# Diagonal products of two heads in one product of 64x128 columns, the unwanted blocks masked when they are collected, and the gram product in another PSUM bank

## The chip, the cores and the metric

The kernel runs on one core of one Trainium2 chip. Its time is the device time in microseconds (us) of one execution, given as the median of several. Lower is better. The core has TensorE (PE, whose weight loads the profile lists as PEld), VectorE (DVE), ScalarE (ACT), GpSimd (POOL) and SyncE (SP, which here issues the DMAs).

## What is computed

A block of a network: layer norm with modulation, a Mamba2 state-space layer, a gated residual, and after it layer norm and a linear layer with binarized weights. The change touches the chunked scan of the state-space layer. Cut to what matters:

```python
def ssd_chunk_scan(X, dA, Bm, Cm, chunk):
    # X: (b,l,h,p), 64 heads h of p = 16; Bm, Cm: (b,l,g,n), 8 groups of n = 64, each shared by 8 heads
    A_cum = jnp.cumsum(A, axis=-1)
    Lm = jnp.exp(segsum(A))                     # lower triangular decays inside a chunk
    Y_diag = jnp.einsum('bcshn,bczhn,bhcsz,bczhp->bcshp', Cm, Bm, Lm, X)
    decay_states = jnp.exp(A_cum[..., -1:] - A_cum)
    states = jnp.einsum('bcshn,bhcs,bcshp->bchpn', Bm, decay_states, X)
    ...
    Y_off = jnp.einsum('bcshn,bchpn,bhcs->bcshp', Cm, states, state_decay_out)
    return (Y_diag + Y_off).reshape(b, l, h, p)
```

Batch is 4, length 512, model width 512, inner width 1024; all in float32.

## The kernel before

The kernel cuts the scan into chunks of 64 tokens. A **step** n is one pair of groups (4 pairs) and one batch element (4): 16 steps, 16 heads and 512 tokens each. A step has 4 **units** u of 128 tokens, that is two chunks c; there are 64 units. The main loop runs over v from -2 to 63 and, in each v, over four slots `sl`. Every engine has its own program, written out in the same slots, and semaphores join them; nothing is scheduled by a tool. In one iteration v PE does, in order: at slot 0 the diagonal and off-diagonal products of unit v and the states and gram products of unit v+1; at slots 1, 2 and 3 the turn of x, two decay products and the turn of B for unit v+2; and in each of the slots 1 to 3 half a projection (`project`, line 1196: six products of 512 columns) of the input for a later step. Between them, in some units, lie turns of weights (`weights`, line 1291).

A unit goes through these stages. `decay` (L1205) makes exponents in bank DB, ACT's `exponent` (L1365) turns them into M; `gram` (L1274) makes C times B for both groups; DVE's `mix` (L1476) multiplies M by it, two operations of 512 columns. `turn_x` (L1214) puts x with tokens on partitions into bank XT, ACT's `spread` (L1373) copies it to Xp, POOL's `weigh` (L1581) scales it to Xw. `turn_b` (L1223) turns B into bank GB and ACT's `copy_b` (L1378) copies it to BTs. `states` (L1247) makes each chunk's own state; DVE's `update` (L1506, L1509) adds it to the faded one that POOL makes (`fade`, L1591). `diagonal` (L1261) multiplies M by Xp; `offdiagonal` (L1234) multiplies the state by C. DVE's `collect` (L1491, L1492, L1494) scales the off-diagonal part by `ea` and adds the diagonal part, into y1, and POOL's `sum_up` (L1609) adds y1 to t1.

A head has only 16 columns and PE writes in strips of 32 partitions. So Xp holds each head in 32 columns, 16 of them zeros: an even head lies in the lower half, an odd one in the upper. Two products, of an even and an odd head, are summed in one strip (`start=(e == 0), stop=(e == 1)`); the zeros keep them apart. The pair of PSUM banks YS holds, in each bank: columns 0 to 127 the diagonal result, 128 to 255 the off-diagonal one, 256 to 383 the states, 384 to 447 the gram. The products with 64 rows use half of the array's rows, and the half (c or q) also decides the bank.

DVE's program in iteration v is: slot 1 `update(v+1, 0)` and `collect(v)`; slot 2 `update(v+1, 1)` and `mix(v+1)` twice; besides, in slots that a table sets, `silu` (L1467) and the three operations of `convolve` (L1446) on a projected tile. A projection k may start when `silu` of tile k-3 has freed its bank (three banks A). The diagonal of v+1 waits for the mixes of v+1.

## Time and profile before

| | |
|---|---|
| time, median of 3 runs | 672.53 us (671.93 to 673.36) |
| span of the profiled execution | 672.7 us |
| mean granted clock of TensorE | 0.976 |
| busy: PE | 624.5 us, 93% |
| busy: DVE | 521.1 us, 77% |
| busy: ACT, POOL | 379.5 us, 56%; 357.3 us, 53% |
| diagonal products (L1261) | 4096 MATMUL records |

The profiled execution's own time is its span. Busy times of PE count products whose ends are modelled and which overlap, so they say where PE works and not how full it is. A product of float32 operands appears as two MATMUL records and two LDWEIGHTS records.

### The profile page before, as it was taken

To read this page: it belongs to the slowest core of one execution; us is meant where nothing else is said; L and a number is where in the kernel's file an instruction comes from. 1 tells how busy PE (TensorE), PEld (TensorE's weight loads), DVE (VectorE), ACT (ScalarE), POOL (GpSimd) and SP (SyncE) were. 2 spreads that over 40 slices of the span, in tenths; PEclk is the share of its full clock that TensorE was granted. 3 is DMA by queue.
4 is the path that set the end of the run, shared out by engine and by line. 5 is a ranking of instruction groups with operands and counts; after the bars stand their busy time and mean duration, and the time that the engine had idled before them with its cause. 6 is when DMAs were issued, how large, how long until landed. Compare 5 with 4: busy or idle time off the path is not lost.

```text
span 672.7 us, 21311 instructions
## 1 busy us (share of the span) xinstructions
PE 624.5 (93%) x8371; PEld 491.5 (73%) x8371; DVE 521.1 (77%) x947; ACT 379.5 (56%) x834; POOL 357.3 (53%) x416
## 2 busy tenths in 40 slices
PE   3887977999999999999999999999978989999995
PEld 1664756777777878778777878777866767888884
DVE  6698689888687887887778878778698466677766
ACT  3776444546646455646545564756664527665555
POOL 5674211626555463754734655447564645767652
PEclk9698889999999999999999999999997999999999
DMA  9743111242321231322122253222323634444411
GB/s 288 234 146 115 47 38 52 70 157 75 117 70 38 97 107 52 101 69 87 67 71 73 78 168 118 69 101 70 101 69 106 215 125 141 145 153 126 126 48 62
DMA packets 61914, 70.52 MB, mean 105 GB/s; under 512 B 13972, under 2 KB 33460, under 8 KB 61816
## 3 DMA queue, kind: packets, MB, share of 16 engines
q1 hardware_dynamic: 61816, 69.17, 32.1%
q8 instruction: 67, 1.10, 0.7%
q14 instruction: 31, 0.25, 0.1%
HBM read 54.45 MB, written 14.70 MB: 103 GB/s over the span
## 4 chain that ended last, share of the span: by engine, by line
PE 75%; DVE 11%; issue 4%; POOL 4%; ACT 3%; DMA 1%; SPq 0%; POOLq 0%; DVEq 0%; ACTq 0%
PE bank L1196 35%; PE bank L1962 11%; PE pair L1261 7%; PE bank L1205 4%; PE bank L1995 3%; PE pair L1234 3%; PE bank L1291 2%; DVE m_cv L1446 2%; PE bank L1214 2%; PE pair L1247 2%; POOL h_lo L428 1%; DVE chain L589 1%; DVE chain L596 1%; DVE m_M L1476 1%; PE pair L1274 1%
## 5 line engine op out<-in xcount | busy, mean ns | idle before, releaser
L1446 DVE SCALAR_TENSOR_TENSOR m_cv<-bank,gpc,m_cv 128x511 f32<-128x511 f32 (+2 forms) x192 | 143.4, 747 | 38.3 <-ACT m_cv L1353 33.6
L1196 PE MATMUL bank<-h_hi,w_hi 128*128 128x512 f32 x384 | 164.6, 429 | 3.6 <-DVE m_xs L1467 1.9
L1196 PE MATMUL bank<-h_hi,w_lo 128*128 128x512 f32 x384 | 153.1, 399 | 0.0
L1196 PE MATMUL bank<-h_lo,w_hi 128*128 128x512 f32 x384 | 152.5, 397 | 0.4 <-issue 0.4
L1353 ACT ACTIVATE m_cv<-bank,gpc 128x512 f32<-128x512 f32 x96 | 72.0, 750 | 79.8 <-PE bank L1196 79.4
L1365 ACT ACTIVATE m_M<-bank 128x512 f32<-128x512 f32 x128 | 76.0, 594 | 66.5 <-PE bank L1205 65.3
L1591 POOL TENSOR_TENSOR m_S<-m_S,m_cd 128x128 f32<-128x128 f32 x96 | 40.0, 416 | 136.9 <-DVE m_S L1509 71.3
L1196 PEld LDWEIGHTS bank<-h_hi,w_hi 128*128 128x128 f32 x384 | 74.0, 193 | 24.4 <-issue 5.5
L1581 POOL TENSOR_TENSOR m_Xw<-m_Xp,wend 128x256 f32<-128x256 f32 x64 | 39.8, 622 | 87.7 <-ACT m_Xp L1373 87.7
L1196 PEld LDWEIGHTS bank<-h_hi,w_lo 128*128 128x128 f32 x384 | 73.4, 191 | 17.5 <-issue 0.6
L1196 PEld LDWEIGHTS bank<-h_lo,w_hi 128*128 128x128 f32 x384 | 73.9, 192 | 12.1 <-issue 0.3
L1476 DVE TENSOR_TENSOR m_M<-m_M,pair 128x512 f32<-128x512 f32 x128 | 81.7, 679 | 0.2 <-issue 0.2
L1261 PEld LDWEIGHTS pair<-m_M,m_Xp 64*32 64x32 f32 x4096 | 45.7, 105 | 25.9 <-issue 25.5
L1261 PE MATMUL pair<-m_M,m_Xp 64*32 64x64 f32 x4096 | 56.3, 225 | 7.9 <-DVE m_M L1476 7.9
L1360 ACT ACTIVATE bank<-m_cv 128x512 f32<-128x512 f32 x96 | 58.4, 608 | 6.3 <-DVE m_cv L1446 6.3
L1816 POOL TENSOR_TENSOR t_y_lo<-h_lo_place,t_y_hi 128x1024 fp32r<-128x1024 f32 x16 | 39.1, 2445 | 39.6 <-ACT t_y_hi L1762 35.1
L1205 PE MATMUL bank<-R,Lm 84*128 84x512 f32 x128 | 57.3, 448 | 1.5 <-ACT m_M L1365 1.5
L1962 PE MATMUL bank<-h_hi,t_y_hi 128*128 128x512 f32 x128 | 51.5, 403 | 1.3 <-POOL t_y_lo L1816 1.3
L1962 PE MATMUL bank<-h_hi,t_y_lo 128*128 128x512 f32 x128 | 50.7, 396 | 0.0
L1962 PE MATMUL bank<-h_lo,t_y_hi 128*128 128x512 f32 x128 | 50.7, 396 | 0.0
L1467 DVE SCALAR_TENSOR_TENSOR m_gate<-bank,m_cv 128x512 f32<-128x512 f32 x32 | 22.1, 690 | 33.3 <-ACT bank L1360 33.3
L1602 POOL TENSOR_TENSOR m_t<-m_xs,m_dd 128x512 f32<-128x512 f32 x32 | 40.6, 1291 | 4.0 <-DMA m_dd<-dd_scratch 3.1
(184 smaller groups left out, 1260.0 us busy)
## 6 DMA issues: line engine op xcount, KB each, us to landing
m_ea<-ea_scratch SPq DMA_DIRECT2D x32, 256.0 KB
m_dd<-dd_scratch SPq DMA_DIRECT2D x32, 256.0 KB
y_scratch<-m_t SPq DMA_DIRECT2D x16, 512.0 KB, 3.4
h_lo_place<-y_scratch SPq DMA_DIRECT2D x16, 512.0 KB, 4.7
p_wm<-in_L_wmod_dram SPq DMA_DIRECT2D x6, 1024.0 KB, 6.9
m_wraw<-in_L_attn_in_proj_w_dram SPq DMA_DIRECT2D x18, 256.0 KB, 3.1
w_lo_place<-in_L_attn_input__dram SPq DMA_DIRECT2D x16, 256.0 KB, 4.9
out_dram<-t_o SPq DMA_DIRECT2D x16, 256.0 KB, 2.4
```

The lines of the kernel that those rows point to most:

```text
L1196: ins = pe.matmul(A[k % 3][:, :], w[:, t, kc, :], h[:, n % NB, kc, :], start=(m == 0), stop=(m == 11))
L1205: pe.matmul(DB[:, :], s.Lm[:, u % 2, q, :], s.R[:, u % 2, q, :], start=True, stop=True).then_inc(d_done, 1)
L1261: ins = pe.matmul(YS[32 * j:32 * j + 32, c, q * Q:(q + 1) * Q], Xp[half, u % 2, HG * q + h, :], M[half, u % 2, q, h * Q:(h + 1) * Q], star ...
L1353: act.activation(cv[:, k % 3, :], A[k % 3][:, :], ACT.Identity, scale=scale, bias=bias).then_inc(lin_done, 1)
L1360: act.activation(A[k % 3][:, :], cv[:, k % 3, :], ACT.Tanh).then_inc(tanh_done, 1)
L1365: act.activation(M[:, u % 2, q, :], DB[:, :], ACT.Exp).then_inc(exp_done, 1)
L1446: ins = dve.scalar_tensor_tensor(out=cv[:, k % 3, lag:], in0=A[k % 3][:, 0:L - lag], scalar=s.gpc[:, gp, o:o + 1], in1=cv[:, k % 3, lag:], ...
L1476: dve.tensor_tensor(m, m, g, ALU.mult).then_inc(m_done, 1)
L1581: pool.tensor_tensor(Xw[:, :, :].rearrange("p q (j e d) -> p (q j) e d", e=2, d=HD), src, w, ALU.mult).then_inc(xw_done, 1)
L1591: pool.tensor_tensor(S1[:, c, :].rearrange("p (h d) -> p h d", h=HG), S[:, (m - 1) % 4, :].rearrange("p (h d) -> p h d", h=HG), cd[:, b // ...
L1602: pool.tensor_tensor(t1[:, q, :], xs[:, n % 2, q, :], dd[:, q, :], ALU.mult).then_inc(t1_done, 1)
L1962: ins = pe.matmul(OB[i][:, :], y[:, i, k, :], w[k], start=(k == 0 and m == 0), stop=(k == KI - 1 and m == 2))
```

## The change

**Diagonal.** Xp loses its padding: `spread` copies 256 columns as they are, 16 to a head. One product takes the 32 columns of two heads as weights and the two heads' 128 columns of M. Its result of 32 partitions by 128 columns has four blocks; the two in which head and head's decays meet are wanted, the other two are not. 16 products of 128 columns take the place of 32 of 64 columns.

**Collecting.** `own_half` is a column of ones and zeros per head's half (two columns: even, odd). `collect` adds the even half's columns times the first, then the odd half's columns times the second, both with a scalar from a column. So there are three operations for two, and four for three in the first unit of a step. y1 is laid out by chunk.

**Banks.** The diagonal result now takes columns 0 to 127 and 256 to 383 in each bank of YS, and the states 384 to 511. The gram moves into bank GB, the turn of B from there into columns 256 to 383 of XT. Both gram halves share one bank now, so q = 1 waits for q = 0 (`g_first`), and PE's order is gram(0), offdiagonal(1), states, offdiagonal(0), gram(1).

```diff
-        ea, y1 = sb("ea", [P, 2, 2, L]), sb("y1", [P, 2, 2, L])
+        ea, y1 = sb("ea", [P, 2, 2, L]), sb("y1", [P, 2, NC, 2, Q])
-        Xp, Xw = sb("Xp", [P, 2, 2 * HG, 32]), sb("Xw", [P, 2, HG * HD])
+        Xp, _, Xw = sb("Xp", [P, 2, 2 * HG * HD]), sb("pad4", [P, 2 * 2 * HG * HD]), sb("Xw", [P, 2, HG * HD])
...
+        dve.wait_ge(konst, 3)
+        dve.tensor_reduce(s.own_half[:, :], s.ident[:, :].rearrange("p (j e d) -> p e j d", e=2, d=HD), AX.XY, ALU.add)
...
-        pool.wait_ge(t_pe, 16)
-        pool.memset(s.Xp[:, :, :, :], 0.0).then_inc(zeroed, 1)
...
-                pe.transpose(GB[:, 0:P], Bt[:, n % 2, tok(u)], s.ident[:, :]).then_inc(bt_done, 1)
+                pe.wait_ge(xp_done, u + 1)
+                pe.transpose(XT[:, 2 * P:3 * P], Bt[:, n % 2, tok(u)], s.ident[:, :]).then_inc(bt_done, 1)
...
             def diagonal(u):
...
                 for q in range(2):
-                    for e in range(2):
-                        for j in range(4):
-                            for c in range(2):
-                                half, h = slice(64 * c, 64 * c + 64), 2 * j + e
-                                ins = pe.matmul(YS[32 * j:32 * j + 32, c, q * Q:(q + 1) * Q], Xp[half, u % 2, HG * q + h, :],
-                                                M[half, u % 2, q, h * Q:(h + 1) * Q], start=(e == 0), stop=(e == 1))
+                    for j in range(4):
+                        for c in range(2):
+                            half, first = slice(64 * c, 64 * c + 64), q * P + 32 * j
+                            ins = pe.matmul(YS[32 * j:32 * j + 32, c, 2 * P * q:2 * P * q + 2 * Q], Xp[half, u % 2, first:first + 32],
+                                            M[half, u % 2, q, 2 * j * Q:2 * (j + 1) * Q], start=True, stop=True)
...
+            def gram(u, q):
+
+                n, group = u // UPS, slice(64 * q, 64 * q + 64)
+                if q == 1:
+                    pe.wait_ge(g_first, u + 1)
+                else:
+                    if u % UPS == 0:
+                        pe.wait_ge(silu_done, TILE_NO[n, 3] + 1)
+                    pe.wait_ge(bt_read, u + 1)
+                    wait(pe, m_done, 2 * u)
                 for c in range(2):
...
+                    ins = pe.matmul(GB[64 * c:64 * c + 64, q * Q:(q + 1) * Q], Bt[group, n % 2, chunk(u, c)],
+                                    Ct[group, n % 2, chunk(u, c)], start=True, stop=True)
+                ins.then_inc((g_first, g_done)[q], 1)
...
                     if v >= 0 and piece_at(slot) is not None:
                         if sl == 3:
-                            pe.wait_ge(xp_done, u + 1)
+                            pe.wait_ge(xp_done, min(u + 1, NU))
+                            pe.wait_ge(bt_read, min(u + 1, NU))
                         weights(piece_at(slot))
...
-                out = Xp[:, u % 2, :, :].rearrange("p (j e) (m d) -> p j (e m) d", e=2, d=HD)[:, :, 0:4:3, :]
-                act.activation(out, XT[:, 0:2 * P].rearrange("p (j e d) -> p j e d", e=2, d=HD), ACT.Copy).then_inc(xp_done, 1)
+                act.activation(Xp[:, u % 2, :], XT[:, 0:2 * P], ACT.Copy).then_inc(xp_done, 1)
...
             def collect(u):
...
-                dve.wait_ge(g_done, min(u + 2, NU))
+                wait(dve, st_done, min(u + 2, NU))
...
                 if i == 0:
...
-                    dve.tensor_copy(dst[:, 0, :, :], own[:, 0, :, :])
+                    dve.tensor_scalar(flat[:, 0:2, :], own[0][:, 0:2, :], s.own_half[:, 0:1], None, ALU.mult).then_inc(yo_scaled, 1)
                 dve.tensor_tensor(dst[:, first:, :, :], off[:, first:, :, :], scale[:, first:, :, :], ALU.mult).then_inc(yo_scaled, 1)
-                dve.wait_ge(yo_scaled, u + 1)
-                dve.tensor_tensor(dst[:, first:, :, :], own[:, first:, :, :], dst[:, first:, :, :], ALU.add).then_inc(y1_done, 1)
+                dve.wait_ge(yo_scaled, 2 * u + n + 2)
+                dve.scalar_tensor_tensor(out=flat[:, 2 * first:, :], in0=own[0][:, 2 * first:, :], scalar=s.own_half[:, 0:1],
+                                         in1=flat[:, 2 * first:, :], op0=ALU.mult, op1=ALU.add).then_inc(yo_scaled, 1)
+                dve.wait_ge(yo_scaled, 2 * u + n + 3)
+                dve.scalar_tensor_tensor(out=flat, in0=own[1], scalar=s.own_half[:, 1:2], in1=flat,
+                                         op0=ALU.mult, op1=ALU.add).then_inc(y1_done, 1)
```

The new code has its own line numbers. PE's program before, at slot 0 of the iteration whose diagonal belongs to unit 29 (`pair` is YS, `bank` any other PSUM bank, in brackets the semaphores that a row waits for):

```order
L1261 MATMUL pair<-m_M,m_Xp 32x64 [waits m_m_done,m_xp_done,m_s_new,m_y1_done]
L1261 MATMUL pair<-m_M,m_Xp 32x64 x31
L1234 MATMUL pair<-m_Ct,m_S 64x64 x8
L1247 MATMUL pair<-m_Xw,m_BTs 64x128 [waits m_bt_read,m_xw_done,m_s_new]
L1247 MATMUL pair<-m_Xw,m_BTs 64x128
L1274 MATMUL pair<-m_Ct,m_Bt 64x64 [waits m_bt_read]
L1274 MATMUL pair<-m_Ct,m_Bt 64x64 x3
L1196 MATMUL bank<-h_hi,w_hi 128x512 [waits p_h_lo_dve,m_silu_done,p_h_lo_pool,p_w_pool]
```

PE's program after, at the same place:

```order
L1262 MATMUL pair<-m_M,m_Xp 32x128 [waits m_m_done,m_xp_done,m_s_new,m_y1_done]
L1262 MATMUL pair<-m_M,m_Xp 32x128 x15
L1277 MATMUL bank<-m_Ct,m_Bt 64x64 [waits m_m_done,m_bt_read]
L1277 MATMUL bank<-m_Ct,m_Bt 64x64
L1235 MATMUL pair<-m_Ct,m_S 64x64 x4
L1249 MATMUL pair<-m_Xw,m_BTs 64x128 [waits m_bt_read,m_xw_done,m_s_new]
L1249 MATMUL pair<-m_Xw,m_BTs 64x128
L1235 MATMUL pair<-m_Ct,m_S 64x64 x4
L1277 MATMUL bank<-m_Ct,m_Bt 64x64 [waits m_g_first]
L1277 MATMUL bank<-m_Ct,m_Bt 64x64
```

The 32 products have become 16, one gram pair stands ahead of the off-diagonals, the other behind them, and the states stand between the two halves of the off-diagonals.

DVE's program before, around `collect` of unit 28, the first of its step (L1506 and L1509 are `update`, L1476 is `mix`, L1467 is `silu`):

```order
L1509 TENSOR_TENSOR m_S<-m_S,pair 128x128 [waits m_g_done,m_s_part,m_yd_done,m_st_done]
L1491 COPY m_y<-pair 128x2x64 [waits m_ea_ready1,m_g_done,m_y_out,m_yo_done,m_yd_done]
L1492 TENSOR_TENSOR m_y<-pair,m_ea 128x2x64
L1494 TENSOR_TENSOR m_y<-pair,m_y 128x2x64 [waits m_yo_scaled]
L1467 SCALAR_TENSOR_TENSOR m_xs<-bank,m_cv 128x512 [waits m_t1_done,m_xt_done,m_tanh_done]
L1509 TENSOR_TENSOR m_S<-m_S,pair 128x128 [waits m_g_done,m_s_part,m_yd_done,m_st_done]
L1476 TENSOR_TENSOR m_M<-m_M,pair 128x512 [waits m_g_done,m_exp_done] x2
```

DVE's program after, at the same place:

```order
L1525 TENSOR_TENSOR m_S<-m_S,pair 128x128 [waits m_yo_done,m_s_part,m_yd_done,m_st_done]
L1503 TENSOR_SCALAR m_y<-pair,p_own_half 128x128 [waits m_ea_ready1,m_st_done,m_y_out,m_yo_done,m_yd_done]
L1504 TENSOR_TENSOR m_y<-pair,m_ea 128x128
L1506 SCALAR_TENSOR_TENSOR m_y<-pair,p_own_half,m_y 128x128 [waits m_yo_scaled]
L1509 SCALAR_TENSOR_TENSOR m_y<-pair,p_own_half,m_y 128x256 [waits m_yo_scaled]
L1477 SCALAR_TENSOR_TENSOR m_xs<-bank,m_cv 128x512 [waits m_t1_done,m_xt_done,m_tanh_done]
L1525 TENSOR_TENSOR m_S<-m_S,pair 128x128 [waits m_yo_done,m_s_part,m_yd_done,m_st_done]
L1486 TENSOR_TENSOR m_M<-m_M,bank 128x512 [waits m_g_done,m_exp_done] x2
```

Between the first update and the SiLU of x stand four operations where three stood, the last one over 256 columns. In the other units of a step it is three for two, all of 256 columns.

## Rows read from the trace of the kernel before

**Rows 1.** The page: span, and the chain that ended last, by engine

```profile
span 672.7 us, 21311 instructions
...
PE 75%; DVE 11%; issue 4%; POOL 4%; ACT 3%; DMA 1%; SPq 0%; POOLq 0%; DVEq 0%; ACTq 0%
```

**Rows 2.** Busy time by stretch: length, engines with instructions, granted clock, DMA

```profile
core 0: us, PE busy (x) PEld busy (x) DVE busy (x) ACT busy (x) POOL busy (x), PEclk, DMA share, GB/s
91.10:119.80 28.70, 23.30 (x359) 17.86 (x357) 27.90 (x49) 14.27 (x31) 6.11 (x11) 1.00 0.15 52
262.00:276.00 14.00, 14.00 (x238) 11.16 (x238) 11.83 (x24) 8.71 (x22) 9.62 (x13) 1.00 0.14 42
489.10:502.20 13.10, 10.33 (x138) 7.81 (x138) 12.86 (x27) 8.91 (x21) 7.48 (x11) 1.00 0.22 76
503.00:512.00 9.00, 8.30 (x116) 6.53 (x103) 8.13 (x16) 3.55 (x9) 4.71 (x5) 0.62 0.04 8
```

**Rows 3.** Timeline of PE: start, length, line, instruction, shapes, count of records

```profile
300.15 0.86 PE L1261 MATMUL pair<-m_M,m_Xp 64*32 64x64 f32 x64
300.94 0.46 PE L1234 MATMUL pair<-m_Ct,m_S 64*64 64x64 f32 x16
...
306.80 0.86 PE L1261 MATMUL pair<-m_M,m_Xp 64*32 64x64 f32 x64
...
313.66 1.00 PE L1261 MATMUL pair<-m_M,m_Xp 64*32 64x64 f32 x64
314.59 0.46 PE L1234 MATMUL pair<-m_Ct,m_S 64*64 64x64 f32 x16
```

**Rows 4.** Busy by stretch, instructions of L1261 alone; (x) is how many are in flight

```profile
300.15:300.23 0.08, 0.07 (x8) 0.08 (x16) 1.00 0.00 0
...
300.34:300.40 0.06, 0.06 (x32) 0.06 (x17) 1.00 0.00 0
...
300.48:300.80 0.32, 0.32 (x51) 0.32 (x31) 1.00 0.00 0
```

**Rows 5.** The same view, instructions of L1247 alone

```profile
301.22:301.33 0.11, 0.10 (x4) 0.11 (x8) 1.00 0.00 0
301.33:301.44 0.11, 0.11 (x8) 0.05 (x4) 1.00 0.00 0
```

**Rows 6.** Timeline of DVE, units 29 and 30

```profile
302.66 0.42 DVE L1492 TENSOR_TENSOR m_y<-pair,m_ea 128x256 f32<-128x256 f32 x1
303.11 0.42 DVE L1494 TENSOR_TENSOR m_y<-pair,m_y 128x256 f32<-128x256 f32 x1
303.45 0.28 DVE L1509 TENSOR_TENSOR m_S<-m_S,pair 128x128 f32<-128x128 f32 x1
303.91 1.28 DVE L1476 TENSOR_TENSOR m_M<-m_M,pair 128x512 f32<-128x512 f32 x2 [0.18 <-issue]
```

**Rows 7.** Groups by form: busy us, mean ns of one, idle before

```profile
L1446 DVE SCALAR_TENSOR_TENSOR m_cv<-bank,gpc,m_cv 128x511 f32<-128x511 f32 x64 | 47.7, 745 | 33.7 <-ACT m_cv L1353 33.6
```

**Rows 8.** Timeline of DVE ahead of the diagonal of unit 29

```profile
294.50 2.32 DVE L1446 SCALAR_TENSOR_TENSOR m_cv<-bank,gpc,m_cv 128x511 f32<-128x511 f32 x3 [1.28 <-ACT m_cv L1353]
...
296.93 0.28 DVE L1491 COPY m_y<-pair 128x128 f32<-128x128 f32 x1
...
297.65 0.68 DVE L1467 SCALAR_TENSOR_TENSOR m_xs<-bank,m_cv 128x512 f32<-128x512 f32 x1
...
298.44 1.27 DVE L1476 TENSOR_TENSOR m_M<-m_M,pair 128x512 f32<-128x512 f32 x2
```

**Rows 9.** Waits of PE: total us, times, longest

```profile
PE pair L1261 <- DVE m_M L1476: 7.9, 5, 3.1
```

**Rows 10.** Timeline of DVE and PE: a bank freed, a projection started

```profile
269.86 0.68 DVE L1467 SCALAR_TENSOR_TENSOR m_xs<-bank,m_cv 128x512 f32<-128x512 f32 x1
...
270.59 0.50 PE L1196 MATMUL bank<-h_hi,w_hi 128*128 128x512 f32 x1
...
298.58 0.48 PE L1196 MATMUL bank<-h_hi,w_hi 128*128 128x512 f32 x1
```

More of the change, by code:

```diff
@@ L1246, in states @@
                         half, group = slice(64 * c, 64 * c + 64), slice(64 * q, 64 * q + 64)
-                        ins = pe.matmul(YS[group, c, 256:384], BTs[half, group], Xw[half, q, :], start=True, stop=True)
+                        ins = pe.matmul(YS[group, c, 384:512], BTs[half, group], Xw[half, q, :], start=True, stop=True)
                 ins.then_inc(st_done, 1)
@@ L1377, in copy_b @@
                 wait(act, st_done, u)
-                act.activation(BTs[:, :], GB[:, 0:P], ACT.Copy).then_inc(bt_read, 1)
+                act.activation(BTs[:, :], XT[:, 2 * P:3 * P], ACT.Copy).then_inc(bt_read, 1)
             def weights(i):
@@ L1401, in scalar @@
             start.scalar(act, linear, tanh)
-            act.wait_ge(start.zeroed, 1)
             for v in range(-2, NU):
```

77 lines of the change are left out of this document (40 added, 37 removed).

## The prediction, made before the changed kernel was run

> **What bounds the kernel now.** I read the page first: the chain that ended last is 75% TensorE and 11% VectorE [rows 1]. That is a mean over stages, so I then read busy times by stretch [rows 2]. There the reader sees two regimes. From 262 to 276 us, which stands for nearly all of the loop (unit 6 at 142 us to unit 56 at 488 us), PE is busy 14.00 of 14.00 us and DVE 11.83: TensorE sets the pace. From 91.1 to 119.8 and from 489.1 to 502.2 us DVE is busy 27.90 of 28.7 and 12.86 of 13.1 us: VectorE sets it (as it does again ahead of unit 6), since the first stretch carries the second half's decay chain and the last one the signs of the FFN weight. The change takes work from TensorE and gives work to VectorE, so the question is how much of each lands in which regime, and whether VectorE has room inside the TensorE-bound one.
>
> **What TensorE saves.** A unit's 32 diagonal products are 64 MATMUL records of 64 columns, from 300.15 until the next block starts at 300.94: 0.79 us [rows 3]. How they run, the counts of records in flight show: eight in the first 0.08 us, thirty-two by 300.40 [rows 4], so eight arrays of 64x32 work at once and each group of eight takes about 0.056 us. That rate isn't held: the second half of the 64 takes from 300.40 to 300.80. Afterwards there are 32 records of 128 columns. Their pace is bounded by the states' products, also 128 columns, where four records start in 0.11 us and the next four 0.11 us later [rows 5], twice the 0.056 of 64 columns. If eight arrays still work at once, 32 records are four groups: the last starts 3 x 0.11 + 0.05 us after the first. From the last start to the next block the trace leaves 0.14 us (300.80 to 300.94), to which the longer stream adds 0.05. Sum 0.57 us, a saving of **0.21 us a unit**. The columns streamed are the same in number; what goes is the slow second half. Bounds: 0.10 if the new order of the block behind costs 0.11 (below), 0.39 if what costs is the record (0.79/64 x 32). I take 0.21, since the pace of 128 columns is read directly. In seven units of the middle the old block takes 0.93 us (313.66 to 314.59) [rows 3], and there 0.14 more goes.
>
> The block behind it has the same products: gram 4, off-diagonal 8, states 4. Before, each kind filled all four arrays of 64x64 at once; now a gram pair fills the two of the upper row half while the off-diagonal four fill the lower, and the other way round at the end. Counted by array the columns are equal, so I cost it at zero if arrays run independently. The new waits on PE I cost at nothing, and name the cover: for m_done the diagonal has just waited; g_first comes with the first gram products and is asked for behind the states and the other off-diagonals; ScalarE copies Xp while PE computes the second decay, and BTs while PE runs half a projection, six products of 512 columns. If that cover went, the half projections queued behind would be late, and with them their activations.
>
> **What VectorE pays.** Each collect gets one more operation and two with a scalar from a column. Before, the two of 256 columns start 0.45 us apart, and the next independent one 0.34 after the second [rows 6]: 0.79 us. The pointer's price: m_cv's operation reads PSUM with such a scalar over 511 columns in 745 ns [rows 7], m_xs's with a constant over 512 in 0.68 [rows 8], so 0.06 us. After: 0.45, then 0.42 + 0.065 + 0.03 (the gap of a dependent operation) = 0.52, then 0.34 + 0.065 = 0.41: 1.38 us, or **+0.59**. In the first unit of a step the three operations are of 128 columns and take 0.72 us (296.93 to 297.65 [rows 8]); with two pointers and a dependent operation of 256 columns more that is +0.13 and +0.52: **+0.65**. Without the pointer's price it is +0.46, which I keep as the lower end.
>
> **Where it lands.** *Start, units 0 to 5:* VectorE-bound except from 120 to 127 us. Collects 0, 1, 2, 4 and 5 lie on its chain: 2 x 0.65 + 3 x 0.59 = 3.1, less one TensorE saving of 0.21: +2.9 us.
>
> *Middle, units 6 to 56, 50 steps.* PE has waited for a mix only five times in 64 units [rows 9]. In three steps of four VectorE is well ahead: the mixes of unit 30 end at 303.91 + 1.28 = 305.19 [rows 6], the diagonal starts at 306.80 [rows 3], and 1.35 us remain after the 0.26 of such a start when it does wait. Each of these steps loses its 0.21: 38 x 0.21 = 8.0, and 7 x 0.14 = 1.0. The fourth is the second unit of a step, 29, 33 and so on. There, from the convolution at 294.50 VectorE runs without a pause through collect of 28 (296.93), SiLU of x (297.65) and the mixes (to 299.71) [rows 8]. Two things wait for it. The projection that takes the freed bank starts at 298.58, 0.25 us after that SiLU ends at 298.33; in unit 25's step it starts 0.05 us after (269.86 + 0.68 to 270.59) [rows 10]. And the diagonal starts at 300.15, 0.43 us after the mixes. Of those 0.26 is again no cover. So of collect's +0.65 only 0.17 to 0.20 is cover here, and nothing in unit 25. The chain begins at an activation before the preceding diagonal, so TensorE's saving doesn't shorten it. The twelve steps lengthen by 0.45 to 0.64 each, which I take at 0.55: +6.6 us. What is late next is m_cv and the mixes of the following unit, with some 0.6 us left of the 1.35. Middle: 6.6 - 8.0 - 1.0 = -2.4 us.
>
> *End:* collects 56 and 57 lie on VectorE's chain again, +1.2; units 61 to 63 save 3 x 0.21 = 0.6; collect 59 before a TensorE wait about +0.1. +0.7 us.
>
> The work at the start costs nothing: own_half's reduction stands ahead of VectorE's wait for the first copy of the decay weight, and is hidden there, and the zeroing of Xp that goes from POOL had idle time behind it. ScalarE's copy and POOL's weighting of 256 columns keep their sizes.
>
> Sum: 2.9 - 2.4 + 0.7 = +1.2 us on a profiled span of 672.7 [rows 1], which is the median of the runs (672.5) within 0.2. **Forecast 673.7 us**: no change that the measurement tells; it tells about 0.2%, 1.35 us.
>
> **Rivals.** *VectorE's extra is cheap (B).* If the pointer costs nothing, the start pays 2.1 instead of 2.9, the middle 12 x 0.36 instead of 6.6, the end 0.3 instead of 0.7: 2.1 + 4.3 - 9.0 + 0.3 = -2.3, **670.2 us**. For it: m_cv's operands also start at odd offsets, which could be its 0.06. Against: its 509 and 511 columns cost the same. Chance 0.18.
>
> *Records cost, not columns (C).* The second half of the 64 records is paced by something per record, for they are no wider than those of the first. If that price holds for all, 32 fewer save 0.39 us a unit: 38 x 0.18 and the end's 0.5 more than above, **666.4 us**. Against it: eight starts in 0.056 us [rows 4]. Chance 0.07. The Trainium skill ("TensorE: Matmul & The Clock Gate", Back-to-back issue gap) gives small products a floor of about 25 ns each. By that the 64 would have taken 1.6 us, where the trace has 0.79 for this tiling, and halving them would save 0.8 us a unit, which I don't believe.
>
> *Arrays don't run apart (D), the slower side.* If PE starts products strictly in order, the states' second product waits for the row half in which the off-diagonals still run, while the other, with only the gram pair, stands idle for one group of 0.11 us; the saving is then 0.10 instead of 0.21 in the 38 steps and four more at the ends: 42 x 0.11 = +4.6, **678.3 us**. Since the forecast already stands at +1.2, it decides from 0.01 us a unit on. For it: nothing in the old order tests unequal halves. Against: eight starts in 0.08 us from products that each are two records on one array [rows 4]. Chance 0.17. The Trainium skill says both: products start in strict order ("TensorE: Matmul & The Clock Gate", Part 3), and arrays work independently ("TensorEngine Tiling (Array Packing)", Key Properties); no run so far decides it.
>
> *Clock (E).* PE now pauses about 0.6 us more per unit in the VectorE-bound stretches. From 489.1 to 502.2 us it was busy 10.33 of 13.1, and from 503 to 512 the granted clock is 0.62, so three quarters of these nine at 1.2 instead of 2.4 GHz [rows 2], which costs up to 3.4 us. One such stretch more, on the path: **676.5 us**. Chance 0.13.
>
> **Numbers.** The forecast (A, its own range 671.5 to 675.8 from the 0.45 to 0.64 of the twelve steps and 0.04 us either way in TensorE's saving) has 0.45, B 0.18, C 0.07, D 0.17, E 0.13. Leaving out C and the far part of D gives 669.3 to 678.0. Of A somewhat more than half lies inside 0.2%. Faster 0.27 (B, C, the edge of A), same 0.34, slower 0.39 (D, E, A's upper part).
>
> **What would show it.** The diagonal block at about 0.57 us from its first record to the gram's, in even groups of eight per 0.11 us; the block behind it unchanged at 0.73 us to the next projection (0.84 under D). Collect at 1.38 us from its first operation to the next. PE idle about 0.5 us once in four units, waiting for m_xs or m_M, where before it was not. Unit 6 about 3 us later than 142.34, unit 56 about where it was. I would be wrong if VectorE's operations with a column scalar cost under 0.45 us, if the block behind the diagonal grows, or if the clock falls elsewhere.

## The result, and the profile after

The changed kernel took **678.12 us** in the median of four runs (676.11 to 681.79), the kernel before beside it 672.71 (671.93 to 673.36): a ratio of 1.0092, interval 1.0063 to 1.0120. The forecast was 673.7 with a range up to 678.0, so the change cost 5.4 us where I expected 1.2. Run again later (e9, six runs), it took 678.10 against 672.49, ratio 1.0072 (1.0047 to 1.0097).

The page of the changed kernel: span, busy times, and the chain that ended last.

```profile
span 679.9 us, 17403 instructions
...
PE 622.1 (92%) x6323; PEld 478.0 (70%) x6323; DVE 554.9 (82%) x1012; ACT 379.8 (56%) x834; POOL 354.6 (52%) x415
...
PE 67%; DVE 17%; issue 6%; ACT 5%; POOL 4%; DVEq 1%; POOLq 0%; ACTq 0%
```

Against [rows 1] the chain has moved from TensorE (75% to 67%) to VectorE (11% to 17%). A share says nothing yet of where. For that I took the first record of a unit's diagonal block (L1261 before, L1262 after) as a milestone and read how far apart the milestones lie in both traces:

| stretch | before | after | difference | forecast |
|---|---|---|---|---|
| start to unit 0 | 94.10 | 96.20 | +2.1 | 0 |
| unit 0 to 6 | 48.24 | 51.39 | +3.15 | +2.9 |
| unit 6 to 8 | 13.52 | 14.71 | +1.2 | -0.4 |
| unit 8 to 56 | 331.76 | 330.56 | -1.2 | -2.0 |
| unit 56 to 63 | 51.69 | 54.75 | +3.1 | +0.9 |
| unit 63 to the end | 133.4 | 132.3 | -1.1 | -0.2 |
| span | 672.7 | 679.9 | +7.2 | +1.2 |

(The forecast's Middle and End are cut at units 8 and 63 here: 48 of its 50 steps hold 36 x 0.21 + 1.0 - 12 x 0.55.) The profiled execution was the longest of the four. At 681.79 us it lies 3.7 us over its kernel's median. In every run of this study the time lies 1.7 to 2.3 us above the span; so the profiled execution of before, with its span of 672.7, must have been about 2 us over its median too. The median's +5.4 is what has to be explained, and the profile's +7.2 holds 1.8 us on top.

**The steady middle.** Busy time by stretch (the columns are those of [rows 2]) from unit 8 to 56, first before the change, then after:

```profile
155.85:487.61 331.76, 331.11 (x5661) 263.06 (x5660) 262.35 (x504) 192.38 (x429) 179.61 (x239) 1.00 0.27 86
```

```profile
162.31:492.87 330.56, 323.12 (x4125) 249.52 (x4124) 287.52 (x553) 192.39 (x429) 179.30 (x239) 1.00 0.27 86
```

And what TensorE waited for in that stretch of the changed kernel (total us, how many times, longest):

```profile
PE bank L1197 <- DVE m_xs L1477: 7.4, 12, 0.9
```

TensorE's busy time falls by 8.0 us and its idle time rises from 0.65 to 7.4: twelve waits in twelve steps, each for SiLU of x, which stands behind the collect. That is the mechanism of the forecast in one view: -8.0 + 6.8 = -1.2.

How the wait comes about shows in VectorE's timeline ahead of unit 29:

```profile
303.29 0.28 DVE L1525 TENSOR_TENSOR m_S<-m_S,pair 128x128 f32<-128x128 f32 x1
303.48 0.35 DVE L1503 TENSOR_SCALAR m_y<-pair,p_own_half 128x128 f32<-128x128 f32 x1
303.74 0.28 DVE L1504 TENSOR_TENSOR m_y<-pair,m_ea 128x128 f32<-128x128 f32 x1
304.06 0.35 DVE L1506 SCALAR_TENSOR_TENSOR m_y<-pair,p_own_half,m_y 128x128 f32<-128x128 f32 x1
304.45 0.48 DVE L1509 SCALAR_TENSOR_TENSOR m_y<-pair,p_own_half,m_y 128x256 f32<-128x256 f32 x1
304.85 0.68 DVE L1477 SCALAR_TENSOR_TENSOR m_xs<-bank,m_cv 128x512 f32<-128x512 f32 x1
```

The collect takes 1.37 us from its first operation to the SiLU, where it took 0.72 [rows 8]: the +0.65 that was forecast for a step's first unit. TensorE's timeline of the same place and of the diagonal blocks of units 28 and 29:

```profile
300.14 0.67 PE L1262 MATMUL pair<-m_M,m_Xp 64*32 64x128 f32 x32
300.74 0.27 PE L1277 MATMUL bank<-m_Ct,m_Bt 64*64 64x64 f32 x2
...
305.58 0.50 PE L1197 MATMUL bank<-h_hi,w_hi 128*128 128x512 f32 x1 [0.35 <-DVE m_xs L1477]
...
307.18 0.67 PE L1262 MATMUL pair<-m_M,m_Xp 64*32 64x128 f32 x32
307.78 0.27 PE L1277 MATMUL bank<-m_Ct,m_Bt 64*64 64x64 f32 x2
...
307.94 0.27 PE L1249 MATMUL pair<-m_Xw,m_BTs 64*64 64x128 f32 x1
307.96 0.22 PE L1235 MATMUL pair<-m_Ct,m_S 64*64 64x64 f32 x1
307.96 0.32 PE L1249 MATMUL pair<-m_Xw,m_BTs 64*64 64x128 f32 x1
...
308.29 0.22 PE L1277 MATMUL bank<-m_Ct,m_Bt 64*64 64x64 f32 x2
308.34 0.23 PE L1235 MATMUL pair<-m_Ct,m_S 64*64 64x64 f32 x2
308.35 0.23 PE L1277 MATMUL bank<-m_Ct,m_Bt 64*64 64x64 f32 x2
308.40 0.22 PE L1235 MATMUL pair<-m_Ct,m_S 64*64 64x64 f32 x1
308.55 0.50 PE L1197 MATMUL bank<-h_hi,w_hi 128*128 128x512 f32 x1
```

The projection waits 0.35 us for the SiLU that ends at 305.53. The diagonal block is 0.60 us long (300.14 to 300.74) where it was 0.79 [rows 3] and 0.57 was forecast. The block behind it, forecast to stay at 0.73, is 0.77 us in unit 29 (307.78 to 308.55): the states' products (L1249) no longer start in even groups but one by one among the off-diagonals (L1235).

**The clock.** What the change lost from unit 6 to 8 is not a wait. Here are the busy times of the changed kernel for the stretch as a whole, then for the part of it in which the clock was down:

```profile
147.59:162.31 14.72, 14.71 (x173) 11.40 (x173) 12.20 (x23) 5.51 (x12) 5.62 (x7) 0.88 0.20 59
147.90:151.30 3.40, 3.40 (x62) 2.61 (x41) 3.33 (x7) 0.00 (x0) 1.31 (x2) 0.50 0.18 64
```

TensorE is busy throughout, and its granted clock is 0.50, that is 1.2 instead of 2.4 GHz, from 147.9 to 151.3. Just before, from 145.10 to 147.59, it had stood idle for the mixes of unit 6. Before the change that pause was 1.65 us (140.69 to 142.34). The diagonal of unit 6, with the pause ahead of it in brackets, first before the change, then after:

```profile
142.34 0.36 PE L1261 MATMUL pair<-m_M,m_Xp 64*32 64x64 f32 x19 [1.65 <-DVE m_M L1476]
```

```profile
147.59 0.92 PE L1262 MATMUL pair<-m_M,m_Xp 64*32 64x128 f32 x32 [2.49 <-DVE m_M L1486]
```

Before the change the same stretch ran at full clock:

```profile
142.34:155.85 13.51, 13.51 (x236) 10.82 (x236) 11.12 (x21) 5.51 (x12) 5.57 (x7) 1.00 0.22 76
```

The profiled executions as wholes show the clock too: mean 0.976 before, 0.962 after.

### The profile page after: what moved, and what is told of

Its sections match the earlier page's. It is cut to its first block, busy times and chain, and to the rows that moved or that the text cites. A ratio compares the mean times of both kernels' runs of the same rounds, so it can differ in the third digit from the quotient of the medians.

```text
span 679.9 us, 17403 instructions
## 1 busy us (share of the span) xinstructions
PE 622.1 (92%) x6323; PEld 478.0 (70%) x6323; DVE 554.9 (82%) x1012; ACT 379.8 (56%) x834; POOL 354.6 (52%) x415
## 4 chain that ended last, share of the span: by engine, by line
PE 67%; DVE 17%; issue 6%; ACT 5%; POOL 4%; DVEq 1%; POOLq 0%; ACTq 0%
PE bank L1197 31%; PE bank L1980 11%; DVE m_cv L1456 5%; PE pair L1262 4%; PE bank L2013 3%; PE bank L1206 3%; PE bank L1294 2%; PE bank L1277 2%; PE pair L1235 2%; ACT m_cv L1365 2%; PE bank L1215 2%; PE pair L1249 1%; DVE m_xs L1477 1%; DVE m_M L1486 1%; PE pair L767 1%
## 5 line engine op out<-in xcount | busy, mean ns | idle before, releaser
L1197 PE MATMUL bank<-h_hi,w_hi 128*128 128x512 f32 x384 | 166.7, 434 | 13.2 <-DVE m_xs L1477 11.8
L1456 DVE SCALAR_TENSOR_TENSOR m_cv<-bank,gpc,m_cv 128x511 f32<-128x511 f32 (+2 forms) x192 | 143.2, 747 | 27.8 <-ACT m_cv L1365 23.2
L1197 PE MATMUL bank<-h_lo,w_hi 128*128 128x512 f32 x384 | 154.4, 402 | 0.0
L1486 DVE TENSOR_TENSOR m_M<-m_M,bank 128x512 f32<-128x512 f32 x128 | 81.6, 679 | 0.0
L1980 PE MATMUL bank<-h_hi,t_y_hi 128*128 128x512 f32 x128 | 51.5, 403 | 1.3 <-POOL t_y_lo L1834 1.3
L1235 PE MATMUL pair<-m_Ct,m_S 64*64 64x64 f32 x896 | 49.2, 227 | 0.0
L1262 PE MATMUL pair<-m_M,m_Xp 64*32 64x128 f32 x2048 | 43.5, 279 | 5.6 <-DVE m_M L1486 5.6
L1277 PE MATMUL bank<-m_Ct,m_Bt 64*64 64x64 f32 x512 | 41.4, 239 | 1.9 <-ACT p_grow L742 1.9
L1262 PEld LDWEIGHTS pair<-m_M,m_Xp 64*32 64x32 f32 x2048 | 26.1, 107 | 23.5 <-issue 23.5
```

Of the source, the lines that this page charges most:

```text
L1197: ins = pe.matmul(A[k % 3][:, :], w[:, t, kc, :], h[:, n % NB, kc, :], start=(m == 0), stop=(m == 11))
L1235: ins = pe.matmul(YS[strip, q, P + Q * c:P + Q * c + Q], S[group, (2 * u + c - 1) % 4, strip], Ct[group, n % 2, chunk(u, c)], start=True, ...
L1262: ins = pe.matmul(YS[32 * j:32 * j + 32, c, 2 * P * q:2 * P * q + 2 * Q], Xp[half, u % 2, first:first + 32], M[half, u % 2, q, 2 * j * Q:2 ...
L1277: ins = pe.matmul(GB[64 * c:64 * c + 64, q * Q:(q + 1) * Q], Bt[group, n % 2, chunk(u, c)], Ct[group, n % 2, chunk(u, c)], start=True, sto ...
L1456: ins = dve.scalar_tensor_tensor(out=cv[:, k % 3, lag:], in0=A[k % 3][:, 0:L - lag], scalar=s.gpc[:, gp, o:o + 1], in1=cv[:, k % 3, lag:], ...
L1486: dve.tensor_tensor(m, m, g, ALU.mult).then_inc(m_done, 1)
```

## The experiments

The theory after the comparison: VectorE's longer collect costs what was forecast, directly; TensorE's saving is smaller, since the block behind the diagonal grew; and TensorE's longer pauses pull its clock down where before they didn't. The rivals: that TensorE's new order, not the collect, gives the saving back (O), and that the clock's falls have nothing to do with the change (chance). Each kernel ran beside the kernel before; ratios are to it, with their 95% intervals. "Unit 8 to 56" and the like are read from each kernel's trace as above.

**e1, TensorE's part alone.** collect is as cheap as before; the rows of odd heads get the unwanted block instead of their own.

```diff
-    dve.tensor_scalar(flat[:, 0:2, :], own[0][:, 0:2, :], s.own_half[:, 0:1], None, ALU.mult)
+    dve.tensor_copy(dst[:, 0, :, :], own[:, 0, :, :])
...
-    dve.scalar_tensor_tensor(out=flat[:, 2 * first:, :], in0=own[0][:, 2 * first:, :], ...)
-    dve.scalar_tensor_tensor(out=flat, in0=own[1], scalar=s.own_half[:, 1:2], in1=flat, ...)
+    dve.tensor_tensor(dst[:, first:, :, :], own[:, first:, :, :], dst[:, first:, :, :], ALU.add)
```

> The changed kernel, whose collect is as cheap as before: three operations without a column scalar, on the even heads' products alone; the odd heads' own-chunk products are computed but not added to y, so the output lacks them. It shows TensorE's part of the change alone. Theory V (the longer collect on VectorE is what costs, directly and through the clock that falls when TensorE pauses): the start's 3.1 us and the twelve lengthened steps go, and the 0.14 us a unit that TensorE's block behind and diagonal save together stays in some 45 units: 672.5 - 6 to 7 = 666 us (664 to 668). Rival O (the new order on TensorE with its waits gives the saving back wherever the collect stands): 671 to 673 us, and the step of the steady group stays at its length of the change.

Measured: 668.74 us against 673.32, ratio 0.9927 (0.9897 to 0.9957), or -4.9 us. Unit 8 to 56 took 325.58 us (-6.2) and unit 0 to 6 47.96 (-0.3). Rival O falls: without the collect's cost the saving stays. The middle saved what was expected (0.14 us in some 45 units); the time is 1 to 2 us above the expected one, and the trace shows where 1.2 of them lie: the clock fell behind the pause before unit 6 here as well (143.2 to 146.6 us; from unit 6 to 8 14.76 us against 13.52), at a pause of 1.88 us. So it isn't the collect alone that brings the fall about.

**e2, VectorE's part alone.** On the kernel before: the column scalars (1.0 and 0.0) and one operation more; y1 is laid out by chunk as in the change.

```diff
-    dve.tensor_tensor(dst[:, first:, :, :], own[:, first:, :, :], dst[:, first:, :, :], ALU.add)
+    dve.scalar_tensor_tensor(out=sums[:, first:, :], in0=whole[:, first:, :], scalar=s.own_half[:, 0:1], ...)
+    dve.scalar_tensor_tensor(out=sums, in0=whole, scalar=s.own_half[:, 1:2], in1=sums, op0=ALU.mult, op1=ALU.add)
```

> The kernel before, whose collect costs what the change's does: the copy and the addition get a column scalar of 1.0, and one more dependent operation of 256 columns adds 0.0 times the product; TensorE's instructions are those of before. Theory V: the start pays 3.1 us, twelve steps 0.45 to 0.64 each (6.6), the end 1.3, and nothing is saved: 672.5 + 11 = 683.5 us (681 to 687, the upper part if TensorE's pauses lower its clock more often). Rival S (VectorE's extra is mostly covered in the middle, and the change loses only by the clock and by TensorE's own waits): 675 to 678 us.

Measured: 684.32 us, ratio 1.0178 (1.0148 to 1.0208), or +12.0 us; 11 was expected, and S falls. Unit 0 to 6: 51.70, +3.5 (forecast 3.1 without TensorE's saving). Unit 6 to 8: 16.36, +2.8, with the clock down from 147.1 us for 6.8 us. Unit 8 to 56: 337.57, +5.8, or 0.48 for each of twelve steps. The busy times of that stretch, and TensorE's wait in it, the same twelve as in the changed kernel:

```profile
163.64:501.21 337.57, 331.91 (x5661) 263.20 (x5660) 288.17 (x553) 192.21 (x429) 179.25 (x239) 1.00 0.27 85
```

```profile
PE bank L1199 <- DVE m_xs L1470: 5.7, 12, 0.7
```

The two halves add up roughly: -4.9 and +12.0 make +7.1, the whole change made +5.4 and +5.6 in its two measurements. In the middle the sum is -6.2 + 5.8 = -0.4 and the whole -1.2.

**e3, SiLU ahead of the collect.** The wait is for SiLU of x; so take it out from behind the collect.

```diff
+    if sl == 1:
+        for k in due(slot, SILU_LAG):
+            silu(k)
     if sl == 1 and v >= 0:
         collect(v)
...
-    for k in due(slot, SILU_LAG):
-        silu(k)
+    if sl != 1:
+        for k in due(slot, SILU_LAG):
+            silu(k)
```

> The changed kernel with the SiLU that falls due in a collect's slot put ahead of that collect on VectorE; the work is the same. The projection that waits for its freed bank then no longer stands behind the collect. Theory V with the bank as the binding wait in the second units of the steps (15 such waits, up to 2.4 us in all of the change's trace): 0.2 to 0.5 us in each of twelve steps, 2.5 to 6 us less than the change: 672 to 676 us. Rival M (the mixes, which keep their place behind both, bind just as much): 677 to 678 us, as the change. A loss, 679 us or more, if the SiLU waits for its tanh and holds the collect up.

Measured: 676.71 us, ratio 1.0066 (1.0042 to 1.0091), not to be told from the change (1.0072 and 1.0092). Unit 8 to 56 took 329.70, 0.9 less than the change. TensorE's waits in that stretch:

```profile
PE pair L1262 <- DVE m_M L1486: 8.4, 12, 0.9
```

Twelve again, but now ahead of the diagonal, that is behind the mixes: rival M in the main, though the time lies between the two that were expected. As in the forecast, two things wait on one chain, and freeing one shows the other.

**e4 and e10, the gram's move alone.** e4 is the kernel before with the gram in GB, the turn of B in XT and the new order on TensorE with its waits; diagonal and collect as before.

```diff
-    offdiagonal(v)
-    states(v + 1)
-    gram(v + 1)
+    gram(v + 1, 0)
+    offdiagonal(v, 1)
+    states(v + 1)
+    offdiagonal(v, 0)
+    gram(v + 1, 1)
```

> The kernel before with the change's other half alone: gram product in the other bank, turn of B in the bank of x's, and the new order behind the diagonal block; the diagonal products stay as before, 64 of 64 columns with padding, and so does collect. Theory K (the skewed halves cost the 0.05 us that the block behind grew by, in every unit that TensorE bounds): 45 to 55 units x 0.05 = +2 to +3: 675 us. Rival D (row halves held back by the order, 0.11 us): 677 to 679 us. Rival N (the growth comes from the longer last diagonal products, not from the order): 672 to 673 us.

Measured: 675.50 us, ratio 1.0041 (1.0014 to 1.0067), or +2.8 us; theory K's figure. Unit 29's block behind the diagonal, from the first gram record to the projection:

```profile
304.62 0.28 PE L1277 MATMUL bank<-m_Ct,m_Bt 64*64 64x64 f32 x2
...
304.79 0.27 PE L1248 MATMUL pair<-m_Xw,m_BTs 64*64 64x128 f32 x1
304.80 0.22 PE L1234 MATMUL pair<-m_Ct,m_S 64*64 64x64 f32 x1
...
305.40 0.50 PE L1196 MATMUL bank<-h_hi,w_hi 128*128 128x512 f32 x1
```

0.78 us, with the same single starts as in the changed kernel, though the diagonal products are the old ones: N falls. What the new order has that the old had not is an unequal load: a gram pair uses each of the two arrays of the upper rows once, the four off-diagonals use each of those of the lower rows twice, and the states' products behind them came in turn from upper, lower, upper, lower rows. e10 turns the two loops and changes nothing else:

```diff
-    for q in range(2):
-        for c in range(2 if u % UPS < UPS - 1 else 1):
+    for c in range(2 if u % UPS < UPS - 1 else 1):
+        for q in range(2):
```

> The kernel of e4 (before, with the gram product moved and the new order, padded diagonal products) with the states' products row half by row half as in e5. Theory K (the alternation of row halves in strict order makes the block 0.05 us longer and is all that the move costs): from the diagonal block to the projection back from 1.562 to 1.515 us, unit 8 to 56 back to 332 us, the time to that of the kernel before, 673.4 us. Rival (the move costs by something else too, its other waits or the turn of B in the other bank): 674.5 to 675.5 us, unit 8 to 56 over 333 us.

The same block in e10:

```profile
300.54 0.27 PE L1277 MATMUL bank<-m_Ct,m_Bt 64*64 64x64 f32 x2
...
300.70 0.28 PE L1248 MATMUL pair<-m_Xw,m_BTs 64*64 64x128 f32 x2
300.71 0.28 PE L1234 MATMUL pair<-m_Ct,m_S 64*64 64x64 f32 x4
...
301.26 0.50 PE L1196 MATMUL bank<-h_hi,w_hi 128*128 128x512 f32 x1
```

Pairs again, and 0.72 us: the loop order makes the 0.05 to 0.06, that is shown. How it does is not. I had counted, for e5, that each product waits for the one ahead of it. But an array's next product of 64 columns starts 0.11 us or more behind the one before it, so that count gives rival D's growth of 0.11. And in the rows of the changed kernel above, records of the second gram pair start at 308.29, while off-diagonal records, which stand ahead of it in the program, start at 308.34 and 308.40.

Unit 8 to 56 went from e4's 334.26 to 330.70. Not all of those 3.6 us are the order: 1.6 of e4's are two single waits (1.0 us that nothing in the profile explains, 0.6 for a load of Lm). TensorE's busy time in the stretch fell by 1.9 us. The whole time, 674.23 us (ratio 1.0026, 1.0006 to 1.0046), overlaps with e4's interval. By the ratios the order costs 1.0 us, within the intervals. e10's time lies between what theory K and its rival gave, 0.26% over the kernel before, while its unit 8 to 56 is shorter than either said, 1.1 us under that of before: whether the move costs anything else stays open. One growth does remain: in a step's first unit the stretch from the diagonal's start to the next projection is 1.51 us before and 1.56 in e4 and e10 alike (means of twelve). No run isolates its cause.

**e5, the same two lines turned in the changed kernel.**

> The changed kernel with one thing turned: the four products of the states come row half by row half (both column halves of the upper rows, then both of the lower) and no longer alternate between the row halves. Counted by 64x64 arrays with starts in strict order, the change's order makes the block behind the diagonal 6 groups of 0.056 us long, since the upper right array waits behind a product of the lower rows; this order makes it 5, as it was before the change. Theory K (that is the 0.05 us by which the moved gram product lengthens each unit, +2.5 us between units 8 and 56): the block shrinks by 0.05 us, the stretch from unit 8 to 56 by 2.0 to 2.7 us, the time to about 675.5 us. Rival G (the growth comes from something else of the move, such as the turn of B in x's bank or the last gram product's own start): no difference from the change, 678 us.

Measured: 675.49 us, ratio 1.0038 (1.0017 to 1.0058), about 2.6 us under the change by the medians. The trace gives less: unit 8 to 56 took 329.60, 0.96 less than the change. Cut by unit of the step (means over units 8 to 55), the stretch from a diagonal's start to the next projection is 1.372, 1.437, 1.376 and 1.502 us in the change (first to fourth unit) and 1.372, 1.391, 1.376 and 1.454 in e5. So the loop order delays two units of four, those where the off-diagonals and the next unit's states are both complete (a step's first unit has half the off-diagonals, and behind its third come half the states). 12 x 0.094 = 1.1 us is what the loop order costs in the middle. My 2.0 to 2.7 took it for every unit.

**e6, keep TensorE busy in two pauses.** Six products of 128x512 into DB, ahead of the diagonals of units 2 and 6, whose results nobody reads.

```diff
+    if v in (2, 6):
+        pe.wait_ge(exp_done, 2 * (v + 2))
+        for _ in range(6):
+            pe.matmul(DB[:, :], s.w_hi[:, 0, 0, :], s.h_hi[:, 0, 0, :], start=True, stop=True)
     if v >= 0:
         diagonal(v)
```

> The changed kernel with six products of 128x512 put on TensorE, into a bank that is free, ahead of the diagonal blocks of units 2 and 6, where TensorE otherwise waits 2.4 to 2.5 us for the mixes; their results are overwritten unread. Theory E (TensorE's pause in the VectorE-bound start lets its clock fall to half right behind it, at 117.2 and 147.9 us of the change's trace, and the second of these costs 1.2 us in the step from unit 6 to 8, 14.7 against 13.5 us before): from 6 to 8 13.4 to 13.6 us, the kernel 1.2 us shorter, 676 to 677 us. Rival (the clock falls at instants that have nothing to do with these two pauses): 14.7 us stay, 678 us.

Measured: 674.66 us, ratio 1.0032 (1.0014 to 1.0051), less than the 676 to 677 that I expected. The pause before unit 6 in TensorE's timeline, and the busy times of the stretch behind it:

```profile
142.85 1.66 PE L1321 MATMUL bank<-h_hi,w_hi 128*128 128x512 f32 x6 [0.47 <-ACT m_M L1381]
144.86 0.67 PE L1262 MATMUL pair<-m_M,m_Xp 64*32 64x128 f32 x32 [0.35 <-DVE m_M L1490]
```

```profile
144.86:158.05 13.19, 13.19 (x172) 10.29 (x172) 12.10 (x23) 5.50 (x12) 5.62 (x7) 1.00 0.18 59
```

13.19 us at clock 1.00 against 14.71 at 0.88: 1.5 us. It is also 0.33 under the 13.52 of before, near the 0.4 that the forecast had for this stretch. The chance theory falls for this place: in all six traces with the long collect on VectorE and this pause left open (after, e2, e3, e5, e8, e9; pauses of 2.35 to 3.03 us) the clock fell within 0.4 us of its end. From unit 0 to 6 another 1.05 us went (50.34 against 51.39); the falls at 117.2 and 147.9 us are gone, one at 102.3 is still there. This 1.05 is less sure: e5's trace, without the six products, has no fall at 117 us either and 50.93 us. So work that does nothing makes the kernel 2.6 us faster by its trace; the medians say 3.4, the ratios 2.7 to 4.0. The median of the mean granted clock is 0.9765 in e6's twelve runs and 0.9695 in the change's six of e9.

**e7, the odd half taken off VectorE.** The experiments point to a version: keep the merged products, mend the order, and let engines with room do the extra operation. ScalarE scales the odd half out of PSUM, GpSimd adds it; ScalarE reads the banks first, and VectorE waits for that.

```diff
+    def odd_half(u):
+        ...
+        act.activation(odd[:, u % 2, :].rearrange("p (r s) -> p r s", s=Q), own, ACT.Copy, scale=s.own_half[:, 1:2])
+    def add_odd(u):
+        ...
+        pool.tensor_tensor(flat, flat, odd[:, u % 2, :], ALU.add)
...
-    dve.scalar_tensor_tensor(out=flat, in0=own[1], scalar=s.own_half[:, 1:2], in1=flat, op0=ALU.mult, op1=ALU.add)
```

> The changed kernel with the states' order of e5 and with the odd heads' half of collect taken off VectorE: ScalarE scales it out of PSUM into SBUF ahead of VectorE's reads of that bank, and GpSimd adds it to y. VectorE keeps three operations a collect as before, one or two of them with a column scalar. Theory V (VectorE's longer collect is what costs): what e1 showed (4.9 us under the kernel before) plus the 2.5 us of the states' order, less 0.5 to 1 for the column scalars: 666 to 667 us. Rival W (VectorE's first operation behind the diagonal block now waits for ScalarE's, 0.4 us and what is queued ahead of it, and this lands on the path in most units as the collect did): 674 to 680 us.

Measured: **667.59 us** against 673.37, ratio 0.9929 (0.9904 to 0.9953): 5.8 us faster than the kernel before and 10 faster than the change, a little over the 666 to 667 that I expected. Busy times from the page, and the two new operations in the groups by line:

```profile
PE 615.5 (92%) x6323; PEld 473.3 (71%) x6323; DVE 529.0 (79%) x948; ACT 406.4 (61%) x898; POOL 400.4 (60%) x479
```

```profile
L1400 ACT ACTIVATE m_odd<-pair,p_own_half 128x256 f32<-128x256 f32 x64 | 30.4, 475 | 51.3 <-PE pair L1241 51.2
...
L1622 POOL TENSOR_TENSOR m_y<-m_y,m_odd 128x256 f32<-128x256 f32 x64 | 47.5, 743 | 4.6 <-DVE m_y L1526 4.6
```

VectorE is busy for 529.0 us where it was 554.9; ScalarE took 30 and GpSimd 48, and both have room. Rival W, that VectorE's first read now waits on ScalarE, stays small: between units 8 and 56 it takes 6.95 us on average from a step's first unit to its second, against 7.46 in the change and 6.88 before.

**e8, e5 and e3 together.**

> The changed kernel with both reorderings: the states by row half (e5) and the SiLU ahead of the collect (e3). If their gains add (2.5 and 1.7 us): 674 us, still no gain over the kernel before. If TensorE's shorter block only lengthens the wait for the mixes in VectorE-bound units, a little less: 675 us. Rival: one of them was chance between runs, 676.5 us.

Measured: 677.80 us (674.19 to 680.92), ratio 1.0073 (1.0048 to 1.0099). Its trace has the shortest middle of all kernels with the long collect (328.70 us), and yet the median is no better than the change's, where 674 to 675 was expected if both gains were real. So the medians confirm neither e3's gain nor, since e8 holds that edit too, e5's 2.6 us; what holds is the 1.1 us that the block's rows show. Its first unit starts at 96.30 us and its clock fell at 35.3, 117.2 and 147.9 us as in the change. Of differences of 1 to 2 us between two medians here no edit need be the cause.

**e9, the change again.**

> The changed kernel once more, unaltered, for more executions and a second profile: its four first ones spread over 5.7 us (676.11 to 681.79), and their times went with their mean granted clocks. Theory E (the extra half-clock stretches in the part before the first unit, at 117 and 148 us, and at 510 to 530 us are partly chance of the execution): the median 676.5 to 677.5 us, the profile's first unit not at 96.2 but nearer to 94.1 to 94.5 us, from unit 8 to 56 330.6 us to within 0.3 as before, from 6 to 8 again 14.7. Rival (all that the first profile shows belongs to the change): 678 us and the same unit times.

Measured: 678.10 us (674.94 to 681.85) and a profile with span 680.0, unit 0 at 96.31 us, unit 0 to 6 51.40, 6 to 8 14.75, 8 to 56 330.56, 56 to 63 54.71. I was wrong about the second profile: it repeats the first to 0.1 us, its half-clock stretches included. But both profiled executions were the longest of their kernel's runs. Time and mean granted clock of the six runs:

```
clock 0.962  0.966  0.968  0.971  0.971  0.976
us    681.85 679.49 676.77 677.78 678.42 674.94
```

Seven us lie between runs of one program, and the longest ones have the lowest clock. The runs of before beside them reach from 0.970 to 0.982 (medians 0.975 and 0.9695).

**e11, e7 with e6's products.**

> The kernel of e7 (odd half scaled by ScalarE and added by GpSimd, states by row half) with e6's six products ahead of the diagonals of units 2 and 6. In e7 the clock fell only behind the first of the two pauses (116.1 to 119.5 us), where VectorE sets the pace; from unit 6 to 8 it took 13.14 us, as e6 with the clock up. Theory E: 0 to 0.5 us less than e7, 667 to 667.6 us. Rival (the extra products delay the diagonal, or what they do for the clock at unit 2 matters more than thought): outside of 666.5 to 668 us.

Measured: 668.11 us, ratio 0.9928 (0.9906 to 0.9950). The time is above the 667 to 667.6 of theory E and just outside the rival's limit of 668; the ratio is that of e7. Unit 6 to 8 took 13.18 us against 13.14: where the clock doesn't fall, the extra products bring nothing. Unit 0 to 6 took 48.39 against 48.88, with e7's fall at 116.1 us gone, but unit 8 to 56 took 325.90 against 324.79.

**The two pauses in all traces.** How long TensorE stood idle for the mixes ahead of the diagonals of units 2 and 6, and when its clock fell, if it did in the pause or within 2 us behind it (all in us, read from the traces as above):

| trace | pause before unit 2 | fall at | pause before unit 6 | fall at |
|---|---|---|---|---|
| before | 3.06 | none | 1.65 | none |
| e10 | 2.98 | none | 1.55 | none |
| e4 | 3.05 | 112.1 | 1.50 | none |
| e1 | 3.24 | 112.5 | 1.88 | 143.2 |
| e7 | 3.36 | 116.1 | 2.02 | none |
| e2 | 2.43 | 116.4 | 2.35 | 147.1 |
| after | 2.40 | 117.2 | 2.49 | 147.9 |
| e9 | 2.42 | 117.3 | 2.49 | 148.0 |
| e5 | 1.21 | none | 2.53 | 145.5 |
| e3 | 3.87 | 112.0 | 2.96 | 146.2 |
| e8 | 3.94 | 117.2 | 3.03 | 147.9 |

Longer pauses before unit 6 go with the fall, yet length alone doesn't decide: one of 1.88 us had a fall behind it and one of 2.02 had none. Before unit 2 the change even has the shorter pause (2.40 against 3.06) and the fall. What decides there stays open.

## Why the prediction was wrong, step by step

- **VectorE's price: right.** 1.37 us for a first unit's collect against 1.37 forecast (0.72 + 0.65). An operation of 256 columns with a column scalar takes 0.48 us (0.42 + 0.065), one of 128 columns 0.35 (0.28 + 0.065).
- **TensorE's saving a unit: right.** The diagonal block takes 0.60 us for the 0.57 forecast, 0.19 less than before.
- **Start, "+2.9": right in size, in part by luck.** It measured +3.15, of which e6's trace gives back 1.05 with one fall of the clock fewer. So VectorE's direct share may be nearer to 2.1, and the clock had the rest; e5's trace puts the clock's share lower.
- **"The twelve steps lengthen by 0.45 to 0.64": right.** From a step's first unit to its second it took 7.46 us on average against 6.88, +0.58. The other three save 0.20, 0.22 and 0.27, against 0.21 and the long blocks' share.
- **"The block behind it ... I cost it at zero": wrong.** This is rival D, in kind but at half the size. D expected a group of 0.11 us in each of 42 units; the loop order costs 0.05 us, and only in two units of four. That is 1.1 us in the middle of the trace; alone on the kernel before, the move cost 2.8 us in the median (interval 0.9 to 4.5). Why the medians show more than the trace stays open, and so does how the order delays the later products. The Trainium skill says ("TensorE: Matmul & The Clock Gate", Part 3) that products start in strict order; the rows of unit 29's block don't show that, since the second gram pair starts at 308.29, ahead of off-diagonal records at 308.34 and 308.40 that the program has before it. The Trainium skill also says ("TensorEngine Tiling (Array Packing)", Key Properties) that arrays work independently; that agrees with eight records of the diagonal in flight in the first 0.06 us (shown below), but not fully with this block, where the loop order alone moved the next projection by 0.05 us (e5, e10).
- **The clock, left to a rival of 0.13: the step that failed most.** I gave a stretch of half clock a price of up to 3.4 us, but put it beside the forecast and not into it: the sum has the clock at nothing. From unit 6 to 8 the change took 14.71 us where the sum has 13.1, at a mean clock of 0.88, behind a pause that had grown from 1.65 to 2.49 us; with that pause filled it took 13.19 (e6). My own sum lengthened this pause, so this was where to look. Filling two such pauses gave back 2.6 us in the trace and 3.4 in the medians. What could be read beforehand was thin, though: in the trace of before no fall stood behind the pause of 1.65 us, and none behind the one of 3.06 before unit 2.
- **"Span 672.7, which is the median of the runs": a wrong reading without effect.** Times lie 1.7 to 2.3 us above spans, so a span isn't to be compared with a median. The forecast is a difference added to a time, and stands.

The median's miss is 5.4 - 1.2 = 4.2 us. Measured one at a time, the two failed steps are worth 2.6 to 3.4 us (clock, e6) and 1.1 to 2.6 (loop order, e5), which would cover it; no run mends both in the changed kernel.

Of the profile's +7.2 us, 5.2 lie before unit 0 and from unit 56 to 63, and both stretches have more half clock than in other traces. Up to unit 0 the traces with 27 us of it take 95.6 to 96.3 us (after, e2, e7, e8, e9, e11) and those with 17 to 21 us take 93.6 to 94.5 (before, e1, e3, e4, e5, e6, e10), although after, e3, e5, e6, e8 and e9 run nearly the same program up to there. From unit 56 to 63 the change has 14 us of it and takes 54.7 us, e5 and e6 have 7 and take 51.5 and 51.7; but e2 has 14 too and takes 52.1. So these 5.2 us can't be put down to the longer collect alone, which e5 and e6 have as well; they go with the clock, in the start closely and at the end roughly. Why one execution falls into such stretches and another doesn't, and how much of it a median run of the change pays, stays open.

## What to carry to other kernels

Work moved from the bounding engine to one that is ahead on average is paid for where the second engine has a chain without slack; count those places, as the mean busy share hides them. Then give the extra operation to whichever engine has room there: e7 keeps the merged products and wins 5.8 us, where the change lost 5.4. On TensorE in small tiles, try the order in which products on different arrays are issued: here two lines of loop order were worth 0.05 us in every second block. And a pause of TensorE cost more than its length where the clock fell behind it (1.5 us from unit 6 to 8), so a sum should hold that term, with a range, wherever it makes a pause longer.
